# A state-space scan on one core: the last sum of delta moved to GpSimd, du's turning and one quad moved behind slot 12

## The chip, the core and the metric

The kernel runs on one core of a Trainium2 chip. The core has TensorE (PE, with its weight loads as PEld), VectorE (DVE), ScalarE (ACT), GpSimd (POOL) and SyncE (SP, which only starts transfers here). Each works through its own list in order and waits on semaphores. The metric is the device time of one execution in microseconds (us); lower is better.

## What is computed

The input is 16 sequences of 256 tokens with 128 features. Four layers of a selective state-space block run one behind the other, then a mixture of experts with a router. The part that the change touches is in the block:

```
def _selective_scan(u, delta, A, Bm, Cm, Dp):
    def step(h, inp):
        u_t, d_t, b_t, c_t = inp
        dA = jnp.exp(d_t[:, :, None] * A)
        h = dA * h + (d_t * u_t)[:, :, None] * b_t[:, None, :]
        y = jnp.einsum('bdn,bn->bd', h, c_t)
        return (h, y)
    ...
    return ys.transpose(1, 0, 2) + u * Dp

def _mamba_block(x, p):
    ...
    xc = jax.nn.silu(_causal_depthwise_conv(xp, p['conv_w'], p['conv_b']))
    dbc = xc @ p['Wx']
    dt, Bm, Cm = jnp.split(dbc, [DT_RANK, DT_RANK + D_STATE], axis=-1)
    delta = jax.nn.softplus(dt @ p['Wdt'] + p['bdt'])
    ...
```

There are 256 inner channels and 16 states to a channel. softplus(v) is made as max(v, 0) plus the logarithm of 1 + exp(-|v|); "the last sum of delta" adds the two.

## The kernel before

The tokens are cut into 8 groups of 512. A step is one group in one layer, 32 steps in all. The function `window(s, i, par)` is run by each engine once for a step; I call one such run a pass. A pass scans step s and at the same time prepares step s+1 (convolution, projections, delta, du). Passes are written in pairs in a loop: in a pass with par = 0, here called even, ACT starts a load of w_pre (866 KB) at slot 8, and in an odd one a smaller load (128 KB) at slot 12. There is also one pass ahead of step 0, which only prepares, and the work of the experts behind the last.

A pass has 16 slots: 4 groups of states (m = slot // 4) by 4 pairs of channel units. What a slot means on each engine:

- PE, `to_channels(s, slot)`: 8 transposes from dbu_t (delta times u times B, by tokens) into one of two PSUM buffers, dbu_ps[slot % 2]. It waits until the scan, or DVE's product, two slots earlier has left that buffer. At slots 0, 4, 8 and 12 it also waits for all outer products of that group of states by POOL (`dbut_pool`) and ACT (`dbut_act`). I write tc0 to tc15 for these.
- ACT, `exps`: the decays exp(delta * A) of the slot from d_rep, two instructions. d_rep is delta copied to the layout of the states by 16 transfers of 128 KB that SP issues (`replicate`) when delta is ready; slot 0 of the next step needs the first 8 of them, slot 1 the others.
- DVE, `scan`: the recurrence, out of decay and dbu_ps. For the slots 0, 4, 6, 8, 12 and 14 DVE also makes the product with C, straight from PSUM; for the other ten POOL makes it one slot later (`times_c`).
- PE, `quad`: four matmuls that sum the products of two slots over the states. Before the change quads follow to_channels at the slots 5, 7, 9, 11, 13, 15, and the last two of a step at slots 1 and 3 of the next pass.

Around slot 8 to 15 the next step's du is made: ACT computes the parts of softplus at slots 7 and 8. DVE makes three instructions behind its product of slot 8 (lines 876, 880 and 884), of which the third, `delta = delta + sp_l`, is the last sum. POOL makes du = delta * xc at slot 10 (line 502) and then the last two outer products of state group 3. PE turns du (`turn_du`, line 1165, 8 transposes) at slot 11, and ACT copies the result to SBUF at slot 14 (`copy_dut`, line 640). From then on POOL and ACT make the outer products of group 0 of the next step. POOL's six calls of `outer` for that stand at slots 12 to 15 with shares 0, 2, 1, 1: at slot 12 the share is empty, but the call waits there all the same:

```
if first == 0:
    wait(pool, dbu_ready, SLOTS * s + PRS * (m - 1))
    if m == 0:
        pool.wait_ge(dut_ready, 2 * (s + 1))
        pool.wait_ge(bt_ready, s + 1)
```

In the next pass, ACT makes xc (line 588) at its slot 3, PE's `project_z` (line 1110) at slot 2 waits for xc since the two share PSUM banks, and ACT's sz waits for project_z. Line 1100 is the convolution, in four pieces at slots 14, 15, 0 and 1.

Of the kernel before, what the change touches and what calls it, by code (L numbers as in the profile page):

```python
# [10 lines left out]
ALU = mybir.AluOpType  # L11
# [12 lines left out]
KT = DI // 128  # L24
# [5 lines left out]
PRS = UNITS // 2  # L30
# [18 lines left out]
FIRST = (0, 3, 6, 8)  # L49
POOL_SHARE = (0, 2, 3, 4, 4)  # L50
POOL_FIRST = (0, 0, 2, 3, 4)

DVE_C = (0, 4, 6, 8, 12, 14)
ND = len(DVE_C)
# [25 lines left out]
def build_program(nc, xT, x_rows, norm_w, Win, conv_w, conv_b, Wx, Wdt, bdt, A_log, Dp, Wblk, Wout, bout,  # L80
                  gate_w, w1, w2, out):
    ctx = ExitStack()
    with ctx:
# [19 lines left out]
        sp_l = sb("sp_l", [128, KT, TG])  # L103
        delta = sb("delta", [128, KT, TG])
# [130 lines left out]
        dve_sp = sem("dve_sp")  # L235
        delta_ready = sem("delta_ready")
# [83 lines left out]
        def has(s, offset):  # L320

            return not isinstance(s, int) or 0 <= s + offset < STEPS
# [120 lines left out]
        def _(pool):  # L443
# [24 lines left out]

            def outer(s, par, m, first, last):

                if first == 0:
                    wait(pool, dbu_ready, SLOTS * s + PRS * (m - 1))
                    if m == 0:
                        pool.wait_ge(dut_ready, 2 * (s + 1))
                        pool.wait_ge(bt_ready, s + 1)
                    if isinstance(s, int) and s == 0 and m < 2:
                        pool.wait_ge(made_stored[m], 16 if m else 2 * 16)
                for q, j in itertools.product(range(first, last), range(POOL_J)):
                    dst = dbu_t[m % 2][:, j, :, q, :]
                    src = du_t[par][:, j, :].rearrange("p (b c) -> p b c", b=UNITS)  # L480
                    col = b_t[par][:, j, q * M + m:q * M + m + 1]
                    if q == 0 and j == 0:
                        nc.gpsimd.tensor_tensor(dst, src, col.unsqueeze(2).broadcast_to([128, UNITS, CH]), ALU.mult)\
                            .then_inc(dbut_pool, 1)
                    else:
                        nc.gpsimd.tensor_scalar(dst, src, col, 1.0, ALU.mult, ALU.mult).then_inc(dbut_pool, 1)  # L486
# [9 lines left out]
            def window(s, i, par):  # L496
                nxt = 1 - par
                for slot in range(SLOTS):
                    m = slot // PRS + 1
                    if slot == 10 and has(s, 1):  # L500
                        pool.wait_ge(delta_ready, s + 2)
                        nc.gpsimd.tensor_tensor(du[:, :, :], delta[:, :, :], xc[nxt][:, :, :], ALU.mult)\  # L502
                            .then_inc(du_ready, 1)
                    if m < M and has(s, 0):
                        outer(s, par, m, POOL_SHARE[slot % PRS], POOL_SHARE[slot % PRS + 1])
                    if m == M and has(s, 1):
                        outer(s + 1, nxt, 0, POOL_FIRST[slot % PRS], POOL_FIRST[slot % PRS + 1])
                    if slot == 0 and has(s, -1) and has(s, 0):
                        times_c(s - 1, i if par else i - 1, nxt, SLOTS - 1)
                    elif slot and has(s, 0) and slot - 1 not in DVE_C:  # L510
                        times_c(s, i, par, slot - 1)
                    if slot == 7 and has(s, 2):
                        normalise(s + 2)
                    if slot == 4 and is_last(s):
                        add_bout(0, 0, 0)
# [289 lines left out]
        def _(dve):  # L805
# [15 lines left out]
            for l in range(LAYERS):  # L821
# [8 lines left out]
                for k in range(KT):  # L830
                    c0 = W_D + 128 * k
                    last = nc.vector.tensor_scalar(pre[l][:, c0:c0 + 128], ident[:, :],  # L832
                                                   dp_col[:, l, k:k + 1], None, ALU.mult)
# [28 lines left out]
            def window(s, i, par):  # L862
                for slot in range(SLOTS):
                    if has(s, 0):
                        scan(s, slot)
                        if slot in DVE_C:
                            times_c(s, i, par, slot)
                    if has(s, -1):
                        if slot == 2:
                            gate(s - 1, 0)  # L870
                        if slot == 4:
                            gate(s - 1, 1)
                    if has(s, 1):
                        if slot == 8:
                            dve.wait_ge(sp_ready, s + 2)
                            nc.vector.scalar_tensor_tensor(out=sp_w[:, :, :], in0=sp_w[:, :, :], scalar=LOG_ADD,
                                                           in1=sp_e[:, :, :], op0=ALU.add, op1=ALU.mult)\
                                .then_inc(dve_sp, 1)
                            dve.wait_ge(dve_sp, 2 * (s + 1) + 1)
                            nc.vector.scalar_tensor_tensor(out=sp_l[:, :, :], in0=sp_l[:, :, :], scalar=LN_ERROR,  # L880
                                                           in1=sp_w[:, :, :], op0=ALU.add, op1=ALU.min)\
                                .then_inc(dve_sp, 1)
                            dve.wait_ge(dve_sp, 2 * (s + 1) + 2)
                            nc.vector.tensor_tensor(delta[:, :, :], delta[:, :, :], sp_l[:, :, :], ALU.add)\  # L884
                                .then_inc(delta_ready, 1)
                    if slot == 9 and not has(s, 0) and has(s, 1):
                        for b in range(Q):
                            dve.wait_ge(first_mm, b + 1)
                            nc.vector.tensor_copy(d_rep[0][:, b, :], y_ps[b % 2][:, :]).then_inc(first_rep, 1)
                    if is_last(s):  # L890
                        if slot == 6:
                            residual(0, 0)
                        if slot == 9:
                            norm1(0, 0)
                        if slot == 14:

                            dve.wait_ge(first_hi, 1)
                            nc.vector.tensor_tensor(y_lo[0], y_ff[0], y_hi[0].bitcast(F32), ALU.subtract)\
                                .then_inc(y_split, 2)
                            first_lo(0)  # L900
                        if slot == 15:
                            times_c(s, i, par, slot)
                            first_lo(1)
                            route_scores(0)
# [150 lines left out]
        def _(pe):  # L1055
# [136 lines left out]
            def window(s, i, par):  # L1192
                nxt = 1 - par
                for slot in range(SLOTS):
# [11 lines left out]
                        project_z(s + 1)  # L1206
                    if slot == 4 and has(s, 0):
                        skip(s, i, par, 0)
                    if has(s, 0) and slot >= 5 and slot % 2:
                        quad(s, (slot - 5) // PRS, (slot - 5) % PRS // 2)  # L1210
                    if slot == 4 and has(s, 1):
                        project_dbc(s + 1, nxt)
                    if slot == 4 and has(s, 2):
# [9 lines left out]
                        project_out(s - 1, i if par else i - 1, nxt)  # L1223
                    if slot == 10 and not has(s, 0) and has(s, 1):
                        replicate_first(0, 2)
                    if slot == 11 and has(s, 1):
                        turn_du(s + 1)
                    if slot == 12 and not has(s, 0) and has(s, 1):
                        replicate_first(2, Q)
# [147 lines left out]
```

## Time and profile before

| | us |
|---|---|
| median of three runs | 2141.58 (2139.24 to 2146.53) |
| the profiled execution | 2140.07 |
| its span, first to last instruction | 2138.3 |
| busy in the span: PE, DVE, ACT, POOL | 1856.2, 1861.6, 1682.8, 1362.5 |
| mean granted clock of PE | 0.954 |

The passes reach from about 50 to 1690 us of the span; behind them come the experts. All that follows is read from two passes in the middle, the odd one whose slot 8 is scanned at 652.22 us and the even one whose slot 8 is scanned at 703.22 us. Four views are used: the timeline (instructions of one engine in order of time, equal neighbours merged, with the idle time before them and what ended it), the groups by line, the chain of work that ended last, and the table of stretches with the granted clock of PE, where 1.00 is 2.4 GHz and 0.50 is 1.2 GHz.

### The profile page before, as it was taken

What the parts mean: (1) busy time and instruction counts of PE and PEld (TensorE: products, weight loads), DVE (VectorE), ACT (ScalarE), POOL (GpSimd) and SP (SyncE); (2) the same over time, 40 slices, a digit from 0 to 9 for tenths busy, and PEclk for the clock granted to TensorE, in tenths of its full rate; (3) what the DMA queues carried; (4) which work ended last, traced back from release to release, by engine and by line L of the source; (5) the groups of instructions that cost most, each with busy time, mean ns of one, the idle gap of its engine ahead of it and who ended that gap; (6) DMA issues with size and microseconds to landing.
All of it is one profiled execution on the core that took longest, in us unless ns stands there. A gap on an engine that the chain in (4) does not pass through costs nothing.

```text
span 2138.3 us, 34563 instructions
## 1 busy us (share of the span) xinstructions
PE 1856.2 (87%) x10816; PEld 1170.8 (55%) x10816; DVE 1861.6 (87%) x1762; ACT 1682.8 (79%) x3053; POOL 1362.5 (64%) x1428
## 2 busy tenths in 40 slices
PE   4788888888888888888888888888887799999998
PEld 1444444444444444444444444444444499989998
DVE  3799999999999999999999999999999987767775
ACT  4899999899999999999999999999898443333333
POOL 2688888888888888887788888888887600000000
PEclk9899999999999999999999999999999999999999
DMA  7323232323232323232333333232323200000000
GB/s 243 84 66 80 63 79 62 79 62 79 62 79 63 79 66 81 66 80 71 76 80 76 80 77 82 68 79 62 79 62 73 84 2 11 11 11 10 10 6 11
DMA packets 72777, 138.41 MB, mean 65 GB/s; under 512 B 13072, under 2 KB 31120, under 8 KB 68112
## 3 DMA queue, kind: packets, MB, share of 16 engines
q1 hardware_dynamic: 66320, 119.28, 23.0%
q10 hardware_dynamic: 6400, 18.42, 3.7%
q8 instruction: 30, 0.49, 0.1%
q14 instruction: 27, 0.22, 0.0%
HBM read 63.85 MB, written 7.74 MB: 33 GB/s over the span
## 4 chain that ended last, share of the span: by engine, by line
PE 59%; ACT 16%; DVE 15%; issue 6%; ACTq 1%; POOL 1%; SPq 1%; DMA 1%; DVEq 0%; POOLq 0%
PE dbu_ps L1087 13%; PE y_ps L1312 11%; PE pre_ps L1100 10%; PE dbu_ps L1286 8%; PE y_ps L1069 7%; DVE scan L844 7%; ACT decay L577 6%; DVE dbu_ps L844 5%; ACT scan L655 3%; PE pre_ps L1110 3%; PE pre_ps L1117 2%; PE pre_ps L1165 2%; DVE scan L854 2%; ACT sp_l L624 2%; PE y_ps L1187 1%
## 5 line engine op out<-in xcount | busy, mean ns | idle before, releaser
L492 POOL TENSOR_TENSOR scan<-scan,c_rep 128x1024 f32<-128x1024 f32 x319 | 754.6, 2371 | 138.3 <-DVE scan L844 120.0
L1087 PE MATMUL dbu_ps<-ident,scan 128*128 128x128 f32 x4096 | 559.2, 282 | 239.3 <-DVE scan L844 170.1
L1087 PEld LDWEIGHTS dbu_ps<-ident,scan 128*128 128x128 f32 x4096 | 473.9, 144 | 508.9 <-DVE scan L844 192.5
L844 DVE TENSOR_TENSOR_SCAN scan<-decay,dbu_ps 128x1024 f32<-128x1024 f32 x320 | 722.7, 2275 | 22.9 <-PE dbu_ps L1087 22.8
L577 ACT ACTIVATE decay<-d_rep,a_cur 128x510 f32<-128x510 f32 x1024 | 667.9, 709 | 60.7 <-ACT dbc L601 16.9
L844 DVE TENSOR_TENSOR_SCAN dbu_ps<-decay,dbu_ps 128x1024 f32<-128x1024 f32 x192 | 438.1, 2282 | 93.4 <-PE dbu_ps L1087 91.2
L655 ACT ACTIVATE scan<-du_t,b_t 128x256 f32<-128x256 f32 x1024 | 445.3, 494 | 1.3 <-PE dbu_ps L1087 0.2
L486 POOL TENSOR_SCALAR scan<-du_t,b_t 128x256 f32<-128x256 f32 x896 | 416.0, 484 | 0.0
L780 ACT ACTIVATE decay<-dbu_ps 128x512 f32<-128x512 f32 x256 | 148.0, 598 | 206.8 <-PE dbu_ps L1286 184.4
L1069 PE MATMUL y_ps<-scan,sel 128*32 128x512 f32 x2048 | 301.0, 663 | 0.0
L1100 PE MATMUL pre_ps<-xn,w_pre 128*128 128x512 f32 x512 | 245.5, 603 | 5.3 <-DVE w_pre L832 5.3
L854 DVE TENSOR_TENSOR scan<-dbu_ps,c_rep 128x1024 f32<-128x1024 f32 x192 | 235.1, 1224 | 9.3 <-DMA c_rep<-c_rows 0.6
L1286 PE MATMUL dbu_ps<-split_all 128*128 128x512 f32 x768 | 191.3, 400 | 3.8 <-DVE split_all L908 3.8
L521 POOL TENSOR_TENSOR sp_e<-sp_e,bout_rep 128x512 f32<-128x512 f32 x8 | 10.6, 1335 | 280.2 <-DMA sp_e<-in_x_rows 280.2
L502 POOL TENSOR_TENSOR sp_l<-delta,xc 128x1024 f32<-128x1024 f32 x32 | 75.3, 2353 | 167.6 <-DVE delta L884 167.6
L1018 DVE TENSOR_TENSOR decay<-decay 128x512 f32<-128x512 f32 x256 | 163.6, 686 | 9.1 <-ACT decay L780 8.1
L1286 PEld LDWEIGHTS dbu_ps<-split_all 128*128 128x128 f32 x768 | 141.2, 190 | 33.0 <-issue 5.5
L1005 DVE SCALAR_TENSOR_TENSOR xc<-y_ps,cw,xc 128x128 f32<-128x128 f32 x256 | 72.2, 344 | 97.2 <-PE y_ps L1312 97.0
L1100 PEld LDWEIGHTS pre_ps<-xn,w_pre 128*128 128x128 f32 x512 | 87.8, 191 | 97.4 <-issue 90.6
L1312 PEld LDWEIGHTS y_ps<-w_pre,decay 128*128 128x128 f32 x1024 | 120.4, 194 | 6.0 <-issue 3.6
L1312 PE MATMUL y_ps<-w_pre,decay 128*128 128x128 f32 x1024 | 120.9, 277 | 2.7 <-DVE decay L1018 2.7
L1312 PEld LDWEIGHTS y_ps<-c_rep,decay 128*128 128x128 f32 x1024 | 118.0, 192 | 1.9
(112 smaller groups left out, 1748.2 us busy)
## 6 DMA issues: line engine op xcount, KB each, us to landing
d_rep<-delta SPq DMA_DIRECT2D x496, 128.0 KB, 2.9
c_rep<-c_rows SPq DMA_DIRECT2D x32, 1024.0 KB
w_pre<-prepared_weights ACTq DMA_DIRECT2D x15, 866.0 KB, 13.4
prepared_weights<-scan SPq DMA_DIRECT2D x3, 1122.0 KB, 11.7
scan<-in_conv_w SPq DMA_DIRECT2D x4, 512.0 KB, 5.0
w_out<-prepared_weights SPq DMA_DIRECT2D x16, 128.0 KB, 12.8
sp_e<-in_x_rows SPq DMA_DIRECT2D x8, 256.0 KB, 3.0
d_rep<-in_w ACTq DMA_DIRECT2D x2, 1024.0 KB, 6.6
```

The source lines that it names most:

```text
L486: nc.gpsimd.tensor_scalar(dst, src, col, 1.0, ALU.mult, ALU.mult).then_inc(dbut_pool, 1)
L492: nc.gpsimd.tensor_tensor(ring[slot % RING], ring[slot % RING], c_rep[par][:, slot // PRS, :].unsqueeze(1).broadcast_to([128, 2, TG]), ALU ...
L577: last = nc.scalar.activation(decay[slot % DEC][:, u, :, 1:], src[:, :, 1:], ACT.Exp, scale=a_cur[:, b, m:m + 1])
L655: nc.scalar.activation(dbu_t[m % 2][:, j, :, q, :], du_t[par][:, j, :].rearrange("p (b c) -> p b c", b=UNITS), ACT.Copy, scale=b_t[par][:, ...
L844: nc.vector.tensor_tensor_scan(states.rearrange("p u t -> p (u t)"), decay[slot % DEC].rearrange("p u a t -> p (u a t)"), dbu_ps[slot % 2] ...
L854: nc.vector.tensor_tensor(ring[slot % RING], states, c_rep[par][:, slot // PRS, :].unsqueeze(1).broadcast_to([128, 2, TG]), ALU.mult).then ...
L1018: nc.vector.tensor_tensor(hid[e % 2][:, c, :], hid[e % 2][:, c, :], hid[e % 2][:, c, :], ALU.mult).then_inc(h2_ready, 1)
L1069: last = nc.tensor.matmul(y_ps[k][CH * j:CH * j + CH, :], sel[:, :], ring[slot % RING][:, j % 2, :], start=False, stop=m == M - 1, skip_gr ...
L1087: last = nc.tensor.transpose(dbu_ps[slot % 2][:, u, 128 * j:128 * j + 128], dbu_t[m % 2][:, j, b, :, :].rearrange("p q c -> p (q c)"), ide ...
L1100: tap = nc.tensor.matmul(o, w_pre[:, c0:c0 + 128], xn[:, :, k:k + SEQ], start=k == 0, stop=k == KC - 1, skip_group_check=True)
L1286: last = nc.tensor.matmul(dst, left[l], right[r], start=start and n == 0, stop=stop and n == len(passes) - 1)
L1312: last = nc.tensor.matmul(moe_ps[e % 2][:, DM * j:DM * j + DM], hid[e % 2][:, c, 128 * j:128 * j + 128], w2_sb[e][:, c, :], start=c == 0, ...
```

## The change

It has three parts.

1. PE's order: the fourth quad of a pass and turn_du, which stood at slot 11, now stand at slot 12, so tc12 comes ahead of both.
2. POOL's `outer` waits for the copies of du only where its share is not empty, so at slot 13 and no more at slot 12. The product of slot 11 stands between.
3. The last sum of delta is made by POOL, right in front of du, and no more by DVE. delta_ready is therefore given by POOL, and SP's 16 copies and POOL's own du wait for that.

```
+QUAD_SLOTS = (5, 7, 9, 12, 13, 15)
...
-                if first == 0:
+                if first == 0 and last:
                     wait(pool, dbu_ready, SLOTS * s + PRS * (m - 1))
...
                     if slot == 10 and has(s, 1):
+                        pool.wait_ge(dve_sp, 2 * (s + 2))
+                        nc.gpsimd.tensor_tensor(delta[:, :, :], delta[:, :, :], sp_l[:, :, :], ALU.add)\
+                            .then_inc(delta_ready, 1)
                         pool.wait_ge(delta_ready, s + 2)
...
-                            dve.wait_ge(dve_sp, 2 * (s + 1) + 2)
-                            nc.vector.tensor_tensor(delta[:, :, :], delta[:, :, :], sp_l[:, :, :], ALU.add)\
-                                .then_inc(delta_ready, 1)
...
-                    if has(s, 0) and slot >= 5 and slot % 2:
-                        quad(s, (slot - 5) // PRS, (slot - 5) % PRS // 2)
+                    if has(s, 0) and slot in QUAD_SLOTS:
+                        pair = QUAD_SLOTS.index(slot)
+                        quad(s, pair // KT, pair % KT)
...
-                    if slot == 11 and has(s, 1):
+                    if slot == 12 and has(s, 1):
                         turn_du(s + 1)
```

PE's list before, from tc11 (first two rows) to tc13 (dbu_ps<-ident,scan is to_channels, y_ps<-scan,sel a quad, pre_ps<-ident,sp_l turn_du):

```order
L1087 MATMUL dbu_ps<-ident,scan 128x128 [waits scan_done]
L1087 MATMUL dbu_ps<-ident,scan 128x128 x7
L1069 MATMUL y_ps<-scan,sel 32x512 [waits hc_pool,hc_dve]
L1069 MATMUL y_ps<-scan,sel 32x512 x3
L1165 MATMUL pre_ps<-ident,sp_l 128x128 [waits bt_ready,du_ready]
L1165 MATMUL pre_ps<-ident,sp_l 128x128 x7
L1087 MATMUL dbu_ps<-ident,scan 128x128 [waits scan_done,dbut_act,dbut_pool]
```

PE's list now, the same place:

```order
L1088 MATMUL dbu_ps<-ident,scan 128x128 [waits scan_done]
L1088 MATMUL dbu_ps<-ident,scan 128x128 x7
L1088 MATMUL dbu_ps<-ident,scan 128x128 [waits scan_done,dbut_act,dbut_pool]
L1088 MATMUL dbu_ps<-ident,scan 128x128 x7
L1070 MATMUL y_ps<-scan,sel 32x512 [waits hc_pool,hc_dve]
L1070 MATMUL y_ps<-scan,sel 32x512 x3
L1166 MATMUL pre_ps<-ident,sp_l 128x128 [waits bt_ready,du_ready]
```

tc12, the row that waits for dbut_act and dbut_pool, has moved ahead of the quad and of turn_du.

POOL's list before, from the two outer products of slot 9 to the first ones of the next step (scan<-scan,c_rep is a product with C, scan<-du_t,b_t an outer product, sp_l<-delta,xc is du):

```order
L486 TENSOR_SCALAR scan<-du_t,b_t 128x8x32 x2
L502 TENSOR_TENSOR sp_l<-delta,xc 128x1024 [waits delta_ready]
L486 TENSOR_SCALAR scan<-du_t,b_t 128x8x32 x2
L492 TENSOR_TENSOR scan<-scan,c_rep 128x1024 [waits scan_done] x2
L492 TENSOR_TENSOR scan<-scan,c_rep 128x1024 [waits bt_ready,scan_done,dut_ready,dbu_ready]
L483 TENSOR_TENSOR scan<-du_t,b_t 128x8x32 [waits bt_ready,dut_ready,dbu_ready]
```

POOL's list now, the same place:

```order
L487 TENSOR_SCALAR scan<-du_t,b_t 128x8x32 x2
L503 TENSOR_TENSOR delta<-delta,sp_l 128x1024 [waits dve_sp]
L506 TENSOR_TENSOR sp_l<-delta,xc 128x1024 [waits delta_ready]
L487 TENSOR_SCALAR scan<-du_t,b_t 128x8x32 x2
L493 TENSOR_TENSOR scan<-scan,c_rep 128x1024 [waits scan_done] x3
L484 TENSOR_TENSOR scan<-du_t,b_t 128x8x32 [waits bt_ready,dut_ready,dbu_ready]
```

The sum of delta stands ahead of du, and the third product with C has lost its wait for dut_ready.

## Rows read from the trace of the kernel before

**Rows 1.** The page, first part: busy us (share of the span) and instructions.
```profile
PE 1856.2 (87%) x10816; PEld 1170.8 (55%) x10816; DVE 1861.6 (87%) x1762; ACT 1682.8 (79%) x3053; POOL 1362.5 (64%) x1428
```
**Rows 2.** Timeline of DVE: start us, us, engine line operation out<-in [idle before <-releaser].
```profile
652.22 2.29 DVE L844 TENSOR_TENSOR_SCAN dbu_ps<-decay,dbu_ps 128x1024 f32<-128x1024 f32 x1 [1.28 <-PE dbu_ps L1087]
...
658.20 1.23 DVE L884 TENSOR_TENSOR delta<-delta,sp_l 128x1024 f32<-128x1024 f32 x1
659.35 6.63 DVE L844 TENSOR_TENSOR_SCAN scan<-decay,dbu_ps 128x1024 f32<-128x1024 f32 x3
...
703.22 2.30 DVE L844 TENSOR_TENSOR_SCAN dbu_ps<-decay,dbu_ps 128x1024 f32<-128x1024 f32 x1 [1.27 <-PE dbu_ps L1087]
...
754.66 2.30 DVE L844 TENSOR_TENSOR_SCAN dbu_ps<-decay,dbu_ps 128x1024 f32<-128x1024 f32 x1 [1.27 <-PE dbu_ps L1087]
```
**Rows 3.** Timeline of PE around slots 11 to 13, slot 0, and project_z.
```profile
677.41 1.03 PE L1087 MATMUL dbu_ps<-ident,scan 128*128 128x128 f32 x8
...
684.61 1.88 PE L1110 MATMUL pre_ps<-xn,w_pre 128*128 128x512 f32 x4
...
712.68 1.97 PE L1087 MATMUL dbu_ps<-ident,scan 128*128 128x128 f32 x8 [4.63 <-DVE scan L844]
714.58 1.94 PE L1069 MATMUL y_ps<-scan,sel 128*32 128x512 f32 x8
716.44 1.36 PE L1165 MATMUL pre_ps<-ident,sp_l 128*128 128x128 f32 x8
717.65 1.91 PE L1087 MATMUL dbu_ps<-ident,scan 128*128 128x128 f32 x16
...
728.85 1.03 PE L1087 MATMUL dbu_ps<-ident,scan 128*128 128x128 f32 x8
```
**Rows 4.** Groups by line: busy us, mean ns, idle before and its releaser.
```profile
L502 POOL TENSOR_TENSOR sp_l<-delta,xc 128x1024 f32<-128x1024 f32 x32 | 75.3, 2353 | 167.6 <-DVE delta L884 167.6
L884 DVE TENSOR_TENSOR delta<-delta,sp_l 128x1024 f32<-128x1024 f32 x32 | 39.2, 1225 | 1.1
```
**Rows 5.** Timeline of POOL in the odd pass, from du to slot 15.
```profile
659.51 2.35 POOL L502 TENSOR_TENSOR sp_l<-delta,xc 128x1024 f32<-128x1024 f32 x1 [5.20 <-DVE delta L884]
661.84 0.94 POOL L486 TENSOR_SCALAR scan<-du_t,b_t 128x256 f32<-128x256 f32 x2
662.74 7.07 POOL L492 TENSOR_TENSOR scan<-scan,c_rep 128x1024 f32<-128x1024 f32 x3
669.76 0.62 POOL L483 TENSOR_TENSOR scan<-du_t,b_t 128x256 f32<-128x256 f32 x1
670.35 2.31 POOL L486 TENSOR_SCALAR scan<-du_t,b_t 128x256 f32<-128x256 f32 x5
673.20 2.38 POOL L492 TENSOR_TENSOR scan<-scan,c_rep 128x1024 f32<-128x1024 f32 x1 [0.53 <-DVE scan L844]
675.55 0.94 POOL L486 TENSOR_SCALAR scan<-du_t,b_t 128x256 f32<-128x256 f32 x2
```
**Rows 6.** Timeline of ACT: copies of du, exps of slot 0, xc.
```profile
666.21 1.06 ACT L640 ACTIVATE du_t<-pre_ps 128x512 f32<-128x512 f32 x2
...
682.69 1.27 ACT L588 ACTIVATE xc<-pre_ps,w_pre 128x512 f32<-128x512 f32 x2
...
718.02 1.06 ACT L640 ACTIVATE du_t<-pre_ps 128x512 f32<-128x512 f32 x2
...
723.38 1.33 ACT L577 ACTIVATE decay<-d_rep,a_cur 128x510 f32<-128x510 f32 x2 [0.53 <-DMA d_rep<-delta]
```
**Rows 7.** Stretches: us, busy PE PEld DVE ACT POOL, PE clock, DMA share, GB/s.
```profile
662.40:665.80 3.40, 3.40 (x17) 1.41 (x16) 3.40 (x2) 3.40 (x7) 3.40 (x3) 0.51 0.99 214
710.20:717.00 6.80, 4.32 (x19) 2.33 (x20) 6.78 (x4) 6.80 (x16) 6.49 (x5) 0.50 1.02 189
```
**Rows 8.** Line 371, the copies of delta: who waited for them (us, times).
```profile
  ACT decay L577: 9.2, 10
```
**Rows 9.** The chain that ended last, ahead of step 0: start us, us, what.
```profile
40.88 1.24 DVE delta L884
```

## The prediction

> **What bounds the kernel now.** I read the page first: no engine is full, PE and DVE are busy for 87% each, POOL for 64% [rows 1]. So the passes are bound by a chain that changes engines, and I followed it in the timelines of two neighbouring passes. I count from t8, the start of slot 8's scan: 652.22 in the odd pass, 703.22 in the even one, 754.66 in the next; the passes last 51.00 and 51.44 us [rows 2]. A gain of 0.01 us in a pass is 0.3 us of the kernel, since 31 passes have the place that changes.
>
> Behind slot 8 DVE makes the three instructions of delta, the last at t8+5.98, so slot 9 is scanned only from t8+7.13 [rows 2]. PE stands still for 4.63 us until that scan is done [rows 3]. Then come tc11, the quad, turn_du and tc12, and only tc12 lets DVE go on. PE is then busy almost without a gap into the next pass. tc0 starts at 677.41 (t8+25.19) in the odd pass and at 728.85 (t8+25.63) in the even one [rows 3]; from there it is 25.81 us to the next t8 in both, 677.41 to 703.22 and 728.85 to 754.66 [rows 2, 3]. So the two passes differ by 0.44 us, and all of it lies between t8 and tc0.
>
> That difference is PE's clock. After the 4.63 us of idling it is granted 0.50, the lower of its two levels, for 3.4 us in the odd pass (662.4 to 665.8), and for 6.8 us in the even one (710.2 to 717.0, of which PE works from 712.68) [rows 7]. tc11 takes 1.97 us there where eight transposes at full clock take 1.03, and the quad takes 1.94 [rows 3].
>
> **Part 3, the sum of delta.** On DVE it costs 1225 ns, on POOL the nearest row, du with the same shape, costs 2353 ns; POOL waited for delta 32 times, 167.6 us in all, 5.2 us a pass [rows 4, 5]. DVE saves 1.15 us a pass (658.20 to 659.35 [rows 2]), 36 us over 31 passes if nothing else held the chain. Something does. The Trainium skill, GPSIMD Engine Reference, section "4.1 Engine selection", speaks against this part: elementwise work with two inputs belongs on VectorE, since GpSimd is about twice as slow. The rows agree on the price (2353 to 1225 is 1.92); by that rule alone delta would be 1.1 us later in each pass, and the kernel some 35 us slower. Which it is depends on who waits for delta.
>
> I follow the changed pass. POOL began du 1.31 us after DVE's sum began (658.20 to 659.51 [rows 2, 5]). The new sum waits for the instruction ahead, which ends at about 658.17, so it starts at about t8+6.03. It takes 2.33; du waits for it on the same engine. What such a wait costs on POOL no row shows: at least nothing, at most the 0.3 us that would come of a whole trip through a semaphore as between DVE and POOL (1.31 less the 1.23 of the sum is 0.08, so 0.3 is generous). I take 0.1: du at t8+8.45. From there POOL's rows can be laid end to end, since nothing they wait for is late any more: du 2.33, two outer products 0.90, three products with C 7.02 (662.74 to 669.76), six outer products 2.90, one product 2.35, two outer products 0.90 [rows 5]: 16.4 us, to t8+24.85. tc0 needs those last outer products: with 0.1 for the semaphore it starts at t8+24.95, against 25.19 and 25.63. The gain is 0.24 us in odd and 0.68 in even passes, 0.46 on average, 31 times: 14 us. So of DVE's 1.15 us less than half is left, because POOL becomes the late one.
>
> In the pass ahead of step 0 nothing covers the sum: the chain runs through it [rows 9], and 2.35 for 1.24 costs 1.1 us once.
>
> **Part 1, PE's order.** tc11 now starts at about t8+8.2 (slot 9's scan begins right behind DVE's second instruction, near t8+5.9, plus 2.3). tc12 doesn't follow it: it waits for the last two outer products of group 3, which POOL makes behind du, ready at t8+11.8. Before, tc12 began at 666.21 and 717.65 (t8+13.99 and 14.43; in the odd pass the copies of du on ACT start at that same moment) [rows 3, 6]. So slot 12 is scanned 2.2 to 2.6 us earlier, and DVE has that as slack, for tc0 is late by POOL.
>
> The quad and turn_du, though, come behind tc12: 0.95 for tc12 (half of 1.91), 1.0 for the quad (half of its 1.94 at the lower clock) and 1.2 for turn_du (716.44 to 717.65, nearly all of it at full clock) [rows 3], so turn_du ends at t8+15.0, where it ended at 717.65 (t8+14.4) or 666.2 (t8+14.0). ACT copies du then; its copies started at t8+13.99 (odd) and t8+14.80 (even) [rows 6]. With the first half turned 0.6 earlier than the second, ACT ends about 0.8 us later in the odd pass and at the same time in the even one. All that ACT does after that moves along, up to xc, for which project_z waits. The slack: xc starts at 682.69, its first half is done some 0.75 later (half of 1.27 and 0.1 for the semaphore), project_z starts at 684.61 [rows 3, 6]: 1.17 us, and 0.24 less in the new pass, 0.93. In the even pass tc0 moves by 0.68, which leaves about 0.5. At full clock, therefore, part 1 costs nothing.
>
> At the lower clock it does. tc12 would be longer by 0.9, the quad by 0.9 and turn_du by about 0.6 (transposes 1.97 against 1.03, quad 1.94 [rows 3]): turn_du 2.4 us later, xc up to 2.0 past the slack. How often? PE idles 3.4 us ahead of tc11 in place of 4.63, works for one or two, and idles again until t8+11.8. In the rows the clock came back 4.1 and 4.3 us after PE began again [rows 3, 7]. Counted from tc11 it is back at t8+12.4 and costs 0.3, inside the slack; counted from tc12 it is low through all three. Rows 7 have one short and one long stretch, so I take every second pass as late, and for a late one half of the 2.0, since the clock also comes back inside the stretch: about 0.95 every second pass, 0.47 a pass, 15 us. This is the term I know least: from 0 to 2.0 us a pass. The Trainium skill, TensorE: Matmul & The Clock Gate, section "What's actually happening", says that the chip's look at PE's activity runs free and isn't set anew by the kernel; the rows agree in so far as two nearly equal passes have stretches of 3.4 and 6.8 us.
>
> **Part 2, POOL's wait.** At slot 12 POOL would stand at t8+16.4 with the copies done at t8+15.9: at full clock the old wait would cost nothing any more. In a late pass the copies end near t8+18 and the old wait would hold the product of slot 11 for up to 2 us. The edit takes that price away; I cost it at nothing.
>
> **Sum.** 2140.07 of the profiled execution (span 2138.3) − 14 + 15 + 1 = 2142. The median of the runs is 1.5 above the profiled one, inside their spread of 7; I leave it at 2142: no change. About 0.3%, 6.4 us, is what a measurement of this kernel can tell from none.
>
> **Rivals.**
>
> *The clock costs nothing (faster).* The idle time ahead of tc11 shrinks by 1.2 us and tc12 comes early; if the clock stays up or is back by tc12, POOL's chain alone sets the pass. For: two short pauses in place of a long one. Against: both pauses together last from about t8+4.8 to t8+11.8 with two us of work at most. It gives 2140 − 14 + 1 = 2127; with 0 or 0.3 for POOL's own wait 2124 to 2133.
>
> *The clock is low in every pass (slower).* If the second pause always keeps it low through turn_du, 0.95 falls on each pass: 31 × (0.95 − 0.46) + 1 = 16, so 2156; with the full 2.0, 2189. It is slower by more than 0.3% from a mean loss of 0.63 us a pass on. For: the 6.8 us stretch [rows 7]. Against: passes that come late shift against the clock, and then get a short one.
>
> *delta's copies come late.* delta is ready 1.27 us later (t8+8.5 for 7.2), and SP's copies behind it. In the even pass exps of slot 0 already wait 0.53 us for them, t8+20.16 [rows 6]; such waits stand 10 times in the trace, 9.2 us in all [rows 8]. The full 1.27 on top of 0.9 of waiting, less a slack to project_z of some 1.0, would cost 1.2 us in those ten passes, against a gain of 0.46 to 0.68: about 12 us, and 2140 + 12 − 14 + 1 = 2139 without the clock, 2154 with it. Against: the DMA engines are full then (0.99 and 1.02 [rows 7]) with w_pre in front, so a later start delays the end by less. This is the rival in which the rule of the Trainium skill named above (GPSIMD Engine Reference, section 4.1) would have its way.
>
> *The change doesn't do what it says:* the wait that part 2 removes would already be gone through the others. That changes no number above.
>
> **Chances.** No change 0.55 (2136 to 2148), the clock free 0.27, clock low or copies late enough to be slower 0.18. The range that leaves out no more than 2 in 10 reaches from 2126 to 2155: it takes in most of the first rival and the moderate form of the second. Faster by over 0.3%: 0.27; within: 0.55; slower: 0.18.
>
> **What would show it.** Right: DVE without line 884, slot 9 scanned at t8+5.9; POOL without a gap from the sum of delta to slot 15; PE waiting for POOL ahead of tc12, and ahead of tc0 in the passes that are not late; tc0 at t8+24.95; passes of two kinds, about 50.8 us and 51.5 to 52. In the late ones PE's clock must be 0.50 at turn_du, ACT must wait for turn_du, and project_z for xc. Wrong: if all passes have 50.8 us, the clock's price was mine alone; if exps of slot 0 wait for d_rep in most passes, it is the copies; if POOL's sum takes much more than 2.35 us or slows DVE's scans beside it, the first term falls.

## Result and profile after

| | us | range |
|---|---|---|
| before, median of 7 | 2139.24 | 2135.45 to 2146.77 |
| after, median of 7 | 2153.19 | 2151.40 to 2157.83 |
| ratio | 1.0068 | 1.0053 to 1.0082 |
| profiled execution of after | 2157.83 | span 2156.0 |

The changed kernel is slower by 0.7%. The time lies inside the range and near its upper end; it is what the rival "the clock is low in every pass" gave (2156), not the forecast. I go through the views in the order of the groups ahead of the prediction. All lines behind 502 have moved: the sum of delta on POOL is L503, du L506, the scan L848, DVE's last instruction for delta L884, to_channels L1088, the quad L1070, turn_du L1166, project_z L1111, the copies of du L644, xc L592.

The page, busy us and instructions, for [rows 1]; then the group of the new sum, for [rows 4]:

```profile
PE 1894.5 (88%) x10816; PEld 1192.5 (55%) x10816; DVE 1830.1 (85%) x1730; ACT 1683.2 (78%) x3053; POOL 1434.4 (67%) x1460
...
L503 POOL TENSOR_TENSOR delta<-delta,sp_l 128x1024 f32<-128x1024 f32 x32 | 75.2, 2351 | 127.7 <-DVE sp_l L884 127.7
```

DVE has 32 instructions and 31.5 us less, POOL 32 instructions and 71.9 us more, as the change says. PE has the same 10816 matmuls as before and is busy for 38.3 us more: nothing was added to it, so its work runs slower. That is the line from which the rest follows.

The timeline of DVE, for [rows 2] (start, length, what, idle time before and its releaser). The first row of each pass is t8:

```profile
656.49 2.30 DVE L848 TENSOR_TENSOR_SCAN dbu_ps<-decay,dbu_ps 128x1024 f32<-128x1024 f32 x1 [1.27 <-PE dbu_ps L1088]
...
708.88 2.30 DVE L848 TENSOR_TENSOR_SCAN dbu_ps<-decay,dbu_ps 128x1024 f32<-128x1024 f32 x1 [1.28 <-PE dbu_ps L1088]
...
713.60 1.23 DVE L884 SCALAR_TENSOR_TENSOR sp_l<-sp_l,sp_w 128x1024 f32<-128x1024 f32 x1
714.74 6.63 DVE L848 TENSOR_TENSOR_SCAN scan<-decay,dbu_ps 128x1024 f32<-128x1024 f32 x3
...
760.40 2.30 DVE L848 TENSOR_TENSOR_SCAN dbu_ps<-decay,dbu_ps 128x1024 f32<-128x1024 f32 x1 [1.28 <-PE dbu_ps L1088]
```

Slot 9 is scanned at t8+5.86 (714.74), where it was t8+7.13. The passes last 52.39 and 51.52 us, against 51.00 and 51.44. Over the trace, from one store of dbc to the next (one in each pass, 29 distances), the mean is 51.99 us, and 51.23 before.

POOL's timeline in the second of these passes, for [rows 5]:

```profile
714.91 2.35 POOL L503 TENSOR_TENSOR delta<-delta,sp_l 128x1024 f32<-128x1024 f32 x1 [3.92 <-DVE sp_l L884]
717.34 2.36 POOL L506 TENSOR_TENSOR sp_l<-delta,xc 128x1024 f32<-128x1024 f32 x1
719.67 0.94 POOL L487 TENSOR_SCALAR scan<-du_t,b_t 128x256 f32<-128x256 f32 x2
720.57 7.03 POOL L493 TENSOR_TENSOR scan<-scan,c_rep 128x1024 f32<-128x1024 f32 x3
...
732.78 0.93 POOL L487 TENSOR_SCALAR scan<-du_t,b_t 128x256 f32<-128x256 f32 x2
```

POOL's sum starts at t8+6.03, du at t8+8.46, and the last outer products end at 733.71, t8+24.83; the prediction had 6.03, 8.45 and 24.85. So the loss is not there.

PE's timeline of both passes, for [rows 3]: tc11, tc12, quad (first pass only), turn_du, tc0, project_z.

```profile
664.69 1.97 PE L1088 MATMUL dbu_ps<-ident,scan 128*128 128x128 f32 x8 [3.37 <-DVE scan L848]
668.36 1.97 PE L1088 MATMUL dbu_ps<-ident,scan 128*128 128x128 f32 x8 [1.71 <-POOL scan L487]
670.26 1.94 PE L1070 MATMUL y_ps<-scan,sel 128*32 128x512 f32 x8
672.13 1.77 PE L1166 MATMUL pre_ps<-ident,sp_l 128*128 128x128 f32 x8
...
682.13 1.04 PE L1088 MATMUL dbu_ps<-ident,scan 128*128 128x128 f32 x8
...
690.16 1.98 PE L1111 MATMUL pre_ps<-xn,w_pre 128*128 128x512 f32 x4 [0.67 <-ACT xc L592]
...
717.08 1.19 PE L1088 MATMUL dbu_ps<-ident,scan 128*128 128x128 f32 x8 [3.37 <-DVE scan L848]
720.74 1.97 PE L1088 MATMUL dbu_ps<-ident,scan 128*128 128x128 f32 x8 [2.47 <-POOL scan L487]
...
724.50 1.20 PE L1166 MATMUL pre_ps<-ident,sp_l 128*128 128x128 f32 x8
...
733.94 1.03 PE L1088 MATMUL dbu_ps<-ident,scan 128*128 128x128 f32 x8
...
741.69 1.99 PE L1111 MATMUL pre_ps<-xn,w_pre 128*128 128x512 f32 x4 [0.39 <-ACT xc L592]
```

PE now stands still twice, 3.37 us ahead of tc11 and 1.71 or 2.47 us ahead of tc12. After the second pause tc12 takes 1.97 us in both passes and the quad 1.94, the times of the lower clock; turn_du takes 1.77 in one pass and 1.20 in the other. The granted clock in these stretches, for [rows 7] (us, busy PE PEld DVE ACT POOL, clock, DMA share, GB/s):

```profile
663.00:669.00 6.00, 2.60 (x11) 2.21 (x12) 5.99 (x3) 6.00 (x14) 5.92 (x5) 0.53 0.52 119
669.00:674.00 5.00, 5.00 (x26) 3.01 (x25) 3.51 (x2) 2.22 (x5) 5.00 (x3) 0.54 0.91 204
717.00:718.00 1.00, 0.92 (x8) 0.86 (x8) 1.00 (x2) 1.00 (x4) 0.92 (x2) 0.97 0.18 35
718.00:724.80 6.80, 4.33 (x20) 2.07 (x19) 5.35 (x3) 5.78 (x11) 6.80 (x5) 0.50 0.86 186
```

In the first pass the clock is at 0.5 from just ahead of tc11 nearly to the end of turn_du, some 10 us. In the second it is up for most of tc11 (1.19 us), falls at about 718.0, shortly before tc11 ends, and stays low for 6.8 us, through the second pause, tc12 and the quad. The whole trace is like this: in every pass of the steps 0 to 29 tc12 takes 1.96 or 1.97 us, and the low stretch around it lasts 6.8 or 10.2 us, where it lasted 3.4 or 6.8 us in all but one pass before. ACT's timeline, copies of du and xc, for [rows 6]:

```profile
673.36 1.17 ACT L644 ACTIVATE du_t<-pre_ps 128x512 f32<-128x512 f32 x2 [2.78 <-PE pre_ps L1166]
...
689.42 1.27 ACT L592 ACTIVATE xc<-pre_ps,w_pre 128x512 f32<-128x512 f32 x2
...
725.38 1.09 ACT L644 ACTIVATE du_t<-pre_ps 128x512 f32<-128x512 f32 x2 [1.60 <-PE pre_ps L1166]
...
740.95 1.27 ACT L592 ACTIVATE xc<-pre_ps,w_pre 128x512 f32<-128x512 f32 x2
```

Before, the copies in both passes began without a wait [rows 6]. Now ACT stands idle for 2.78 and 1.60 us, and xc begins at t8+32.93 and t8+32.07, where it was t8+30.47 in the odd pass before. In every pass of the steps 0 to 30 ACT waits more than 1 us for turn_du. The waits of the whole kernel show the sum of it, and they answer to [rows 8] (who waits for whom: us, times, longest):

```profile
ACT du_t L644 <- PE pre_ps L1166: 72.3, 37, 9.6
PE dbu_ps L1088 <- POOL scan L487: 70.2, 39, 3.7
...
PEld pre_ps L1111 <- ACT xc L592: 32.0, 59, 2.3
...
ACT decay L581 <- DMA d_rep<-delta: 6.0, 5, 2.2
```

The first and the third of them before:

```profile
ACT du_t L640 <- PE pre_ps L1165: 10.3, 9, 8.4
PEld pre_ps L1110 <- ACT xc L588: 7.2, 6, 4.6
```

Of the 10.3 us before, 8.4 were a single wait at the start. The waits for the copies of delta have become fewer: 6.0 us, 5 times, where the same view of the kernel before has 13.8 us, 11 times.

### The profile page after: what moved, and what is told of

It reads as the page before. It is cut to its first block and busy times, and to the rows that moved or that the text cites. A ratio compares the mean times of both kernels' runs of the same rounds, so it can differ in the third digit from the quotient of the medians.

```text
span 2156.0 us, 34499 instructions
## 1 busy us (share of the span) xinstructions
PE 1894.5 (88%) x10816; PEld 1192.5 (55%) x10816; DVE 1830.1 (85%) x1730; ACT 1683.2 (78%) x3053; POOL 1434.4 (67%) x1460
## 5 line engine op out<-in xcount | busy, mean ns | idle before, releaser
L1088 PE MATMUL dbu_ps<-ident,scan 128*128 128x128 f32 x4096 | 595.7, 293 | 205.6 <-DVE scan L848 128.6
L1088 PEld LDWEIGHTS dbu_ps<-ident,scan 128*128 128x128 f32 x4096 | 497.8, 150 | 488.5 <-issue 268.4
L848 DVE TENSOR_TENSOR_SCAN scan<-decay,dbu_ps 128x1024 f32<-128x1024 f32 x320 | 723.3, 2277 | 47.3 <-PE dbu_ps L1088 46.9
L581 ACT ACTIVATE decay<-d_rep,a_cur 128x510 f32<-128x510 f32 x1024 | 667.7, 710 | 43.9 <-ACT sp_l L628 10.3
L848 DVE TENSOR_TENSOR_SCAN dbu_ps<-decay,dbu_ps 128x1024 f32<-128x1024 f32 x192 | 439.0, 2286 | 117.2 <-PE dbu_ps L1088 107.3
L1070 PE MATMUL y_ps<-scan,sel 128*32 128x512 f32 x2048 | 297.8, 657 | 0.0
L503 POOL TENSOR_TENSOR delta<-delta,sp_l 128x1024 f32<-128x1024 f32 x32 | 75.2, 2351 | 127.7 <-DVE sp_l L884 127.7
## 6 DMA issues: line engine op xcount, KB each, us to landing
prepared_weights<-scan SPq DMA_DIRECT2D x3, 1122.0 KB, 13.8
w_out<-prepared_weights SPq DMA_DIRECT2D x16, 128.0 KB, 12.8
```

The lines of the kernel that those rows point to most:

```text
L581: last = nc.scalar.activation(decay[slot % DEC][:, u, :, 1:], src[:, :, 1:], ACT.Exp, scale=a_cur[:, b, m:m + 1])
L848: nc.vector.tensor_tensor_scan(states.rearrange("p u t -> p (u t)"), decay[slot % DEC].rearrange("p u a t -> p (u a t)"), dbu_ps[slot % 2] ...
L1070: last = nc.tensor.matmul(y_ps[k][CH * j:CH * j + CH, :], sel[:, :], ring[slot % RING][:, j % 2, :], start=False, stop=m == M - 1, skip_gr ...
L1088: last = nc.tensor.transpose(dbu_ps[slot % 2][:, u, 128 * j:128 * j + 128], dbu_t[m % 2][:, j, b, :, :].rearrange("p q c -> p (q c)"), ide ...
```

## Experiments

Three theories. **A:** the price is turn_du's place behind tc12 in a stretch in which PE's clock is low; with the clock up, the place costs nothing. **B:** the place alone is the price, at any clock. **C:** the sum on POOL is the price, through du or the copies of delta. Each time is a median, and each ratio is to the kernel before on the same chip.

**e1_order_back: parts 2 and 3 without part 1.**

```
-QUAD_SLOTS = (5, 7, 9, 12, 13, 15)
+QUAD_SLOTS = (5, 7, 9, 11, 13, 15)
...
-                    if slot == 12 and has(s, 1):
+                    if slot == 11 and has(s, 1):
                         turn_du(s + 1)
```

> The changed kernel with PE's order of before: quad and turn_du at slot 11, ahead of tc12; POOL still makes the last sum of delta and waits one slot later. Theory A (turn_du stands behind tc12 in a stretch in which PE's clock is low, so ACT's copies of du, xc and project_z come late): the copies no more wait 2 us a pass, POOL's chain alone sets the pass, 2127 us (2120 to 2134). Theory B (the position of turn_du behind tc12 costs at any clock): also 2120 to 2134. Theory C (delta, and with it its 16 copies and du, is too late by 1.3 us because POOL is the slower engine): nothing gained, 2148 to 2157.

Measured: 2127.27 us, ratio 0.9952 (0.9933 to 0.9971), passes of 50.92 us in the mean. PE's timeline, from tc11 to tc12 and tc13 (one row of 16), then tc0:

```profile
652.03 1.59 PE L1088 MATMUL dbu_ps<-ident,scan 128*128 128x128 f32 x8 [3.38 <-DVE scan L848]
653.54 1.94 PE L1070 MATMUL y_ps<-scan,sel 128*32 128x512 f32 x8
655.41 1.30 PE L1166 MATMUL pre_ps<-ident,sp_l 128*128 128x128 f32 x8
656.55 1.91 PE L1088 MATMUL dbu_ps<-ident,scan 128*128 128x128 f32 x16
...
668.82 1.09 PE L1088 MATMUL dbu_ps<-ident,scan 128*128 128x128 f32 x8 [0.90 <-POOL scan L487]
```

The quad and turn_du fill the time in which PE otherwise waits a second time; the clock is low for most of tc11, for the quad and for the start of turn_du, ACT waits for turn_du once in the whole trace (9.6 us, at the start), and tc0 waits for POOL. C falls: the sum on POOL makes the kernel 0.5% faster when part 1 is away. Between A and B this run doesn't decide.

**e2_sum_on_dve: parts 1 and 2 without part 3.**

```
-                        pool.wait_ge(dve_sp, 2 * (s + 2))
-                        nc.gpsimd.tensor_tensor(delta[:, :, :], delta[:, :, :], sp_l[:, :, :], ALU.add)\
-                            .then_inc(delta_ready, 1)
...
+                            dve.wait_ge(dve_sp, 2 * (s + 1) + 2)
+                            nc.vector.tensor_tensor(delta[:, :, :], delta[:, :, :], sp_l[:, :, :], ALU.add)\
+                                .then_inc(delta_ready, 1)
```

> The changed kernel with the last sum of delta back on DVE: PE's new order and POOL's later wait stay. Theory A: PE idles 4.6 us ahead of tc11 again, the clock is low at tc12, the quad and turn_du, ACT's copies wait 1 to 2 us a pass: 2140 to 2155. Theory B: the same, 2140 to 2155. Theory C: delta is early again, so no slower than before, 2125 to 2140.

Measured: 2135.56 us, ratio 0.9981 (0.9967 to 0.9995). That is outside the ranges of A and B and inside that of C, which e1 has refuted; the new order is not slow by itself. PE's timeline shows why; tc11, tc12, turn_du, tc0, project_z:

```profile
661.12 1.97 PE L1088 MATMUL dbu_ps<-ident,scan 128*128 128x128 f32 x8 [4.63 <-DVE scan L845]
663.30 1.97 PE L1088 MATMUL dbu_ps<-ident,scan 128*128 128x128 f32 x8 [0.21 <-DVE scan L845]
...
666.84 1.09 PE L1166 MATMUL pre_ps<-ident,sp_l 128*128 128x128 f32 x8
...
676.17 1.03 PE L1088 MATMUL dbu_ps<-ident,scan 128*128 128x128 f32 x8
...
684.34 1.98 PE L1111 MATMUL pre_ps<-xn,w_pre 128*128 128x512 f32 x4 [0.81 <-ACT xc L589]
```

With the sum on DVE, slot 9 is scanned later, so tc11 comes at t8+9.46 (t8 is 651.66), and tc12's inputs are there as soon as tc11 is done: one pause of 4.63 us and then 0.21, in place of two. The clock is back at turn_du (1.09 us). But it was low for tc11, tc12 and most of the quad, and what A expected of ACT did come; its wait for turn_du stands in every pass:

```profile
ACT du_t L641 <- PE pre_ps L1166: 54.6, 32, 7.7
```

Behind tc0 this costs as much as in the change: from tc0 to the next t8 it takes 26.88 us here, 26.75 and 26.46 in the two passes of the change, 25.81 before. What e2 has and the change lacks is an early tc0, which pays for it: t8+24.51, some 0.7 to 1.1 earlier than before. The two passes here last 51.39 and 50.87 us. So the loss needs parts 1 and 3 together. Part 1 makes the copies of du late at the low clock, with the sum on either engine. Part 3 puts a second pause of PE ahead of tc12, since tc11 comes earlier and the outer products that tc12 needs come later, and it lets POOL come to tc0 no earlier than t8+24.96 (e8, below), so little is left to pay for the late copies.

**e3_repeat and e8_repeat_again: the changed kernel, with PE kept at work.** to_channels makes its transposes four times at slot 10 and twice at slot 11, the same values to the same place in PSUM. The order of all else stays that of the changed kernel.

```
-                for u in range(2):
+                for again, u in itertools.product(range({10: 4, 11: 2}.get(slot, 1)), range(2)):
```

> The changed kernel, but PE makes the transposes of slot 10 four times and those of slot 11 twice, into the same place, so that it hardly idles from slot 10 to 12; nothing else changes. Theory A: the granted clock stays at 1.00 through turn_du, ACT's wait for turn_du falls from 2 us a pass to below 0.5, 2127 us (2120 to 2136), although PE does more. Theory B: the wait stays, 2150 to 2160. Theory C: 2150 to 2160.

Measured: 2127.95 us, ratio 0.9949 (0.9931 to 0.9966). The same kernel ran a second time, for its trace:

> The changed kernel with the transposes of slot 10 four times and of slot 11 twice, once more, for its trace: 2128 us; granted clock 1.00 from slot 10 to turn_du, ACT's wait for turn_du below 0.5 us a pass, project_z hardly waiting for xc, PE waiting for POOL ahead of tc0.

Measured: 2125.93 us, ratio 0.9933 (0.9909 to 0.9957), passes of 50.83 us. PE's timeline: tc10 (four times), tc12, turn_du, tc0:

```profile
644.04 3.66 PE L1088 MATMUL dbu_ps<-ident,scan 128*128 128x128 f32 x32
...
652.12 1.09 PE L1088 MATMUL dbu_ps<-ident,scan 128*128 128x128 f32 x8 [1.71 <-POOL scan L487]
...
654.14 1.09 PE L1166 MATMUL pre_ps<-ident,sp_l 128*128 128x128 f32 x8
...
665.21 1.09 PE L1088 MATMUL dbu_ps<-ident,scan 128*128 128x128 f32 x8 [1.58 <-POOL scan L487]
```

The granted clock from 645 to 652, and from 652 to 660:

```profile
645.00:652.00 7.00, 4.66 (x41) 4.20 (x39) 7.00 (x4) 7.00 (x16) 5.64 (x5) 1.00 0.48 119
...
652.00:660.00 8.00, 7.88 (x55) 4.86 (x56) 7.38 (x5) 7.29 (x15) 8.00 (x6) 1.00 0.93 205
```

This decides between A and B. The order is that of the changed kernel, PE has more to do, the clock stays at 1.00, and the kernel is 1.3% faster than without the repeats (2125.93 to 2153.19; ratios to the kernel before 0.9933 and 1.0068). Eight transposes take 1.09 us where they took 1.97, turn_du ends at t8+14.98 (t8 is 640.25), and tc0 waits for POOL. ACT's waits for turn_du are 18.6 us in all, and 9.4 of that is the one at the start. B falls.

**e4_turn_first: turn_du ahead of the quad, both still behind tc12.**

```
+                    if slot == 12 and has(s, 1):
+                        turn_du(s + 1)
                     if has(s, 0) and slot in QUAD_SLOTS:
...
-                    if slot == 12 and has(s, 1):
-                        turn_du(s + 1)
```

> The changed kernel with turn_du directly behind tc12 and the quad of that slot behind it. Theory A: the quad's 1.9 us at the low clock leave the path of turn_du: ACT waits about 1.9 us less, 2135 us (2127 to 2143). Theory B: 1.0 us (the quad at full clock) is won, less than half of the loss comes back: 2140 to 2150. Theory C: 2150 to 2157.

Measured: 2136.07 us, ratio 0.9981 (0.9968 to 0.9993). PE's tc12 and turn_du still run at the low clock (1.97 and 1.92 us), but turn_du ends a quad earlier; ACT's waits for it fall from 72.3 to 26.4 us and project_z's weight loads wait 7.2 us for xc in place of 32.0. That is the second half of A's chain: how late turn_du ends decides what is lost behind tc0. The rest of the loss stays, ahead of tc0: behind the slow tc12, turn_du and quad PE comes to tc0 at 675.99, t8+25.39 (t8 is 650.60), where it is t8+24.96 in e8.

**e5_before_warm, e6_dve_warm, e7_back_warm: the same repeats in three other kernels.** If the clock costs the changed kernel so much, it may cost the others too. e5 is the kernel before with tc10's transposes made five times; e6 is e2 with five times at slot 10 and twice at 11; e7 is e1 with four times at slot 10.

```
+                for again, u in itertools.product(range({10: 5}.get(slot, 1)), range(2)):
```

> The kernel before, but PE makes the transposes of slot 10 five times into the same place, so that it hardly idles ahead of tc11. Theory A (PE's low clock over tc11, the quad and turn_du sets the pass of the kernel before): with the clock at 1.00 the stretch from tc11 to tc12 loses 1.4 to 1.9 us and the pass about 1 us: 2109 us (2100 to 2122). Theory B (order alone, the clock doesn't matter): 2136 to 2142.

> The changed kernel with the last sum of delta back on DVE, and PE kept busy: the transposes of slot 10 five times, those of slot 11 twice. Theory A: without the low clock neither turn_du nor POOL is late, and the sum on POOL would have been the bound: 2100 us (2090 to 2115), the fastest so far. Theory B: 2130 to 2138, as the same kernel without the repeats (2136).

> The changed kernel with PE's order of before (2127 us) and the transposes of slot 10 four times. Theory A with POOL's chain as the bound that is left (sum of delta, du and all behind them without a gap, 18.9 us from DVE's second instruction to tc0): the clock has nothing more to give, 2127 us (2122 to 2130). Rival: the clock still holds that kernel: 2105 to 2118.

Measured: e5 2104.27 us, ratio 0.9827 (0.9798 to 0.9857); e6 2103.39, 0.9818 (0.9789 to 0.9847); e7 2127.15, 0.9931 (0.9905 to 0.9958). e7 gains nothing over e1: with the sum on POOL a pass has 50.8 us with the low clock (50.85 in the one of e1 that is shown) and without it (50.83 in e8), since tc0 waits for POOL's chain in both. e5 and e6 go below it. e6 differs beyond the intervals neither from e5 nor from e10 (below), which lacks only part 1: with the clock up, part 1 costs nothing that these runs show, which speaks against B once more. In e5, whose t8 is 635.58, POOL's du and its last outer products of slot 15:

```profile
642.87 2.36 POOL L502 TENSOR_TENSOR sp_l<-delta,xc 128x1024 f32<-128x1024 f32 x1 [5.19 <-DVE delta L884]
...
658.33 0.93 POOL L486 TENSOR_SCALAR scan<-du_t,b_t 128x256 f32<-128x256 f32 x2
```

du starts at t8+7.29 and POOL is done at t8+23.68; tc0 follows at 659.38, t8+23.80, and the pass has 49.67 us. With the sum on POOL the same point is at t8+24.83. So of the 1.16 us a pass between e8 and that pass, 1.15 are POOL's slower sum. The next pass of e5 has 50.48 us, like nearly every second one. In it ACT's copies of du begin 0.8 us later, at t8+14.82 (t8 is 685.25), and run from 700.07 to 701.13, and POOL's third product and tc0 wait:

```profile
701.28 2.37 POOL L492 TENSOR_TENSOR scan<-scan,c_rep 128x1024 f32<-128x1024 f32 x1 [0.81 <-DVE dbu_ps L844]
...
709.87 1.09 PE L1087 MATMUL dbu_ps<-ident,scan 128*128 128x128 f32 x8 [0.76 <-POOL scan L486]
```

The view puts POOL's wait down to DVE. But this product is the one that also waits for the copies of du at slot 12, it starts 0.15 us behind them, and in the pass before, in which the copies end 0.8 us earlier, it starts without a gap. So this is the wait that part 2 takes away.

**e9_sum_alone: part 3 alone** (e1 with `if first == 0:` again).

> The kernel before with the third part alone: POOL makes the last sum of delta; PE's order and POOL's wait at slot 12 as before. Theory A: turn_du stands ahead of tc12 again, du's copies are done before POOL comes to slot 12, so the old wait costs nothing and POOL's chain sets the pass: 2127 us (2123 to 2132), as with the second part. Rival: the second part is worth something of its own, 2132 to 2145.

Measured: 2127.34 us, ratio 0.9950 (0.9932 to 0.9967), as e1. Part 2 is worth nothing beside part 3 in the old order. No run has parts 1 and 3 with the old wait.

**e10_wait_warm: part 2 on the kernel before, with the repeats of e5.**

> The kernel before with the second part alone (POOL's later wait) and the transposes of slot 10 five times. Theory A: as e5_before_warm, 2104 us, or below it, since with the sum on DVE POOL comes to slot 12 before the copies of du: 2097 us (2090 to 2106). Rival: the wait costs nothing there either, 2102 to 2107.

Measured: 2100.38 us (2094.12 to 2103.09), ratio 0.9821 (0.9798 to 0.9844). The kernel is 1.8% faster than the one before. In its trace POOL's gap is gone: in the pass whose t8 is 784.59 the three products follow one another, tc0 comes at 808.36, t8+23.77, and the pass has 49.80 us where e5 has 50.48. Other passes wait longer for the copies of delta than in e5 (12.8 us, 9 times, for 9.9 us, 6 times), and the intervals of the two ratios overlap, so that part 2 makes the kernel faster isn't shown.

All together, ratios to the kernel before:

| sum of delta | quad and turn_du at 11 | at 12 | at 11, clock kept up | at 12, clock kept up |
|---|---|---|---|---|
| on DVE | 1 | 0.9981 (e2) | 0.9827 (e5) | 0.9818 (e6) |
| on POOL | 0.9950 (e9), 0.9952 (e1) | 1.0068 (the change) | 0.9931 (e7) | 0.9949 (e3), 0.9933 (e8) |

The mean granted clock of the profiled executions is 0.954 before, 0.936 for the change, 0.941 for e2 and e4, 0.961 and 0.964 for e1 and e9, 0.986 to 0.992 with the repeats. It doesn't order the times: e2 and e4 have a lower clock than the kernel before and are no slower, and e7 and e8 have nearly that of e5 and e6 and are 1% slower. What counts is which work runs at the low clock, and what waits for that work.

## Why the prediction was right or wrong

The median lies inside the stated range, but the forecast, no change, did not come: the kernel is 0.7% slower. The terms at full clock were right. The term of the low clock, +15 us, was less than half of what was measured, about +34 us, and that 2153 still falls inside is owed to the width of the range and in part to a shorter start of the kernel, which nothing in the working foresaw; the profiled execution, 2157.83, lies outside.

**Part 3, POOL's chain: right.** Each station lies within 0.1 us of the forecast, and the gain it promised, 0.46 us a pass, is 0.40 where nothing hides it (51.23 before to 50.83 in e8). The first rival, "the clock costs nothing", had 2127 for this alone; e1, e9 and e3 measured 2127.27, 2127.34 and 2127.95. POOL's wait for its own sum, taken as 0.1, is 0.08 (714.91 + 2.35 = 717.26 to 717.34). The rule of the Trainium skill, GPSIMD Engine Reference, section "4.1 Engine selection", against elementwise work on GpSimd: at the clock as it was, the runs are against it (e9, 0.5% faster); with the clock up they are for it (e5 to e8, 1% slower on POOL). Which engine is better depended on what else was late.

**Part 1 at full clock: right.** tc11 at t8+8.2 and tc12 at t8+11.8 came at t8+8.20 and t8+11.87; turn_du's end, t8+15.0 at full clock, is t8+14.98 in e8, and no time is lost there (e8, and e6 against e10).

**Part 1 at the lower clock: the step that failed.** turn_du's end at that clock, 2.4 us later, came in the first pass, at t8+17.41 (672.13 + 1.77), and nearly in the second, at t8+16.82 (724.50 + 1.20). But the prediction took every second pass as late and gave a late one 0.95 us, 0.47 a pass in the mean, 15 us in all. Measured, every pass is late, and the mean loss is 51.99 − 50.83 = 1.16 us, 34 us over 29 passes: 1.56 in the first of the two passes shown and 0.69 in the second. Two things went into that. First, the count: two passes with stretches of 3.4 and 6.8 us [rows 7] were read as "late or not", though the second pause that the change makes was itself in the working ("idles again until t8+11.8"); the row that would have spoken was that one pause already had the clock down in both passes [rows 3, 7]. Second, the size: the sum let POOL set tc0 in all passes. In the first pass it doesn't: PE has no pause between tc12 at 668.36 and tc0 at 682.13, so tc0 comes at t8+25.64, by PE's own arrears, instead of t8+24.96, where POOL sets it in e8; another 0.9 us comes behind tc0, where project_z waits for xc (26.75 us from tc0 to the next t8, against 25.81). Over the passes of the steps 1 to 28, tc0 comes 0.32 us later than in e8 in the mean (25.29 for 24.97), and the way from tc0 to the next t8 takes 0.86 us more (26.73 for 25.87).

**Part 2: right, as far as it was tested.** It was costed at nothing, and nothing is what e9 against e1 shows.

**The sum again, with what was measured.** Between the two profiled executions lie 17.8 us (2140.07 to 2157.83). 29 distances of passes give 29 × (51.99 − 51.23) = +22.0, which is −0.40 for POOL's chain and +1.16 for the clock, each 29 times. The start gives back: up to the third store of dbc, the first of those counted, it is 3.8 us shorter (124.86 for 128.67), although the sum ahead of step 0 costs 1.16 there (PE waits 8.85 us for delta in place of 7.69; predicted 1.1). In the first pass before, project_z waited 4.32 us for xc and then took 3.78 us, twice its usual time; after has no such wait. Ahead of that, ACT waited 4.61 us for the copies of delta before and 0.46 after. But this wait is anywhere from 0.72 to 6.14 us in the traces of the other kernels with the sum on DVE and from 1.07 to 4.45 us in those with it on POOL, so it isn't shown that the change made the start shorter. With medians the difference is 13.95 us.

**Rivals.** "The clock is low in every pass" is what happened, with a price of 1.16 in place of 0.95 and some 4 us less at the start; it shared a chance of 0.18 with the late copies. "delta's copies come late" is refuted: 5 waits, 6.0 us. Of "the change doesn't do what it says", one piece holds: in the old order the wait that part 2 removes costs nothing beside part 3 (e9). What the forecast lacked as a rival is that two parts, each good or harmless alone (0.9950 and 0.9981), hurt together.

## What to carry to other kernels

Before a short piece of work is moved behind a wait, look at what it did where it stood: the quad and turn_du were PE's filling between two waits, and behind the second wait tc12 and most of the quad ran at the low clock in every pass. Where a row of matmuls takes twice its usual time behind a pause, cost the slow rows as well as the pause, and try filling the pause with harmless work: here repeated transposes made the kernel before 1.7% faster. The mean clock doesn't show such a price; the rows and their waits do. A slower engine may take over work as long as its own chain is not the next bound; lay that chain end to end, as here, and again when the other bound is gone.

## What was not expected of the hardware

- Two pauses of 3.37 and 1.71 us with 1.97 us of work between them left PE at the clock of 0.5 for some 10 us, 5 us of them with PE at work without a gap (669.00 to 674.00: busy 5.00, clock 0.54). In the next pass, with a second pause of 2.47 us, it was 6.8 us.
- Transposes can keep the clock up. In e5, 40 of them (4.53 us) stand in PE's long pause; with tc11 behind them PE does nothing else from 639.37 to 646.06, and the granted clock is 1.00 from 640 to 646 and from 646 to 654. In the kernel before it falls to 0.50 at the same place [rows 7]. The Trainium skill, TensorE: Matmul & The Clock Gate, section "Part 4: PE-mode transpose", says that the full clock does not engage for transposes. The runs here show otherwise for these fp32 transposes, and they decide.

```profile
639.37 4.53 PE L1087 MATMUL dbu_ps<-ident,scan 128*128 128x128 f32 x40
...
640.00:646.00 6.00, 4.87 (x44) 4.52 (x42) 5.93 (x5) 6.00 (x15) 3.13 (x3) 1.00 0.49 119
```

- The low clock was a price of the kernel before as well: with PE's long pause filled it is 1.7% faster (e5), though PE was busy for 87% of the span and stood still for 4.63 us in one place of a pass.
- A POOL instruction that waits for the POOL instruction right ahead of it starts 0.08 us after it (two places: 717.34 behind 717.26, and in e8 648.72 behind 648.64).
